# The last of four graph layers rebuilt: its edge keys spread by TensorE and compared on all partitions

## The reference, cut to what matters

```python
h = jnp.maximum(_layernorm(x, axis=-1), 0.0)
x = x + _L3_gnn_ref(h, L3_gnn_rel_embed_weight, L3_gnn_W, src, edge_type_64, dst)

def _L3_gnn_ref(entity_emb, rel_embed_weight, W, heads, rels, tails):
    e_h = entity_emb[heads]
    e_t = entity_emb[tails]
    e_r = rel_embed_weight[rels]                      # 64 relation types
    score = jnp.sum(e_t * jnp.tanh(e_h + e_r), axis=-1)
    score_exp = jnp.exp(score - lax.stop_gradient(jnp.max(score)))
    score_sum = jax.ops.segment_sum(score_exp, heads, num_segments=n_entities)
    attn = score_exp / (score_sum[heads] + 1e-10)
    agg = jax.ops.segment_sum(attn[:, None] * e_t, heads, num_segments=n_entities)
    return jax.nn.leaky_relu((entity_emb + agg) @ W.T, negative_slope=0.2)
```

## Time and profile before

| what | us |
| --- | --- |
| median of 3 runs | 12000.18 |
| lowest and highest of them | 11999.4, 12002.33 |
| the profiled execution | 12014.41 |
| its span in the trace | 12012.6 |
| layer 3's group loop in it, from the last clearing of `a_far` to the last sum | 9146.9 to 11893.4 |

### The profile page before, as it was taken

The page is one execution under the profiler, slowest core; times in us unless marked ns, Lnnn a source line. Parts: engine busy times, 40 slices in busy tenths (PEclk is TensorE's granted clock), DMA queues, the critical chain, the costliest instruction groups (busy, mean ns, idle before and its releaser), DMA issues. The chain is left out here.

```text
span 12012.6 us, 257271 instructions
## 1 busy us (share of the span) xinstructions
PE 8140.2 (68%) x63022; PEld 6349.2 (53%) x63685; DVE 8287.7 (69%) x33874; ACT 4862.3 (40%) x9481; POOL 6896.0 (57%) x7087
## 2 busy tenths in 40 slices
PE   0222222255888888867766777777755999999996
PEld 0222222234566555556545666666653777777775
DVE  7444444426888888878526999999987666666664
ACT  3000000003777777722103555555542444444442
POOL 1777777722777777720004777777753666666662
PEclk9999999998888888889857999999987999999997
DMA  3333333330222222146301222222252333333345
GB/s 116 80 80 80 80 80 80 78 29 24 61 60 59 59 58 58 50 121 175 104 11 34 60 59 60 60 59 60 60 46 64 98 99 98 98 99 98 98 97 59
DMA packets 863125, 886.04 MB, mean 74 GB/s; under 512 B 466669, under 2 KB 636430, under 8 KB 862693
## 3 DMA queue, kind: packets, MB, share of 16 engines
q0 software_dynamic: 254464, 511.95, 18.7%
q1 hardware_dynamic: 608613, 373.57, 12.0%
HBM read 699.65 MB, written 155.84 MB: 71 GB/s over the span
## 5 line engine op out<-in xcount | busy, mean ns | idle before, releaser
L1291 POOL DMA_INDIRECT a_far<-node_table,a_rows x3552 | 3464.3, 975 | 3242.7 <-DMA a_rows<-edge_records 1256.1
L1069 POOL DMA_INDIRECT message_records<-f_msg,f_index x1760 | 1746.3, 992 | 924.2 <-issue 528.1
L897 POOL DMA_INDIRECT sum_far<-split_table,sum_rows x1760 | 1669.2, 948 | 669.4 <-issue 631.9
L982 PE MATMUL banks<-sum_far,sum_hot 128*128 128x128 bf16 x5280 | 635.5, 310 | 1711.8 <-DMA sum_far<-split_table,sum_rows 1604.8
L982 PEld LDWEIGHTS banks<-sum_far,sum_hot 128*128 128x128 bf16 x5280 | 528.2, 143 | 1819.0 <-issue 891.1
L964 ACT ACTIVATE acc<-sum_cur 128x128 f32 x880 | 272.2, 309 | 2752.8 <-DVE sum_cur L926 2415.6
L926 DVE SCALAR_TENSOR_TENSOR sum_cur<-sum_cur,gsame,banks 128x128 f32<-128x128 f32 x880 | 303.0, 344 | 1253.6 <-PE banks L982 1250.5
L1429 PE MATMUL banks<-ident,a_score 128*128 128x128 f32 x7072 | 997.1, 287 | 223.2 <-DVE a_score L1351 197.5
L1449 PE MATMUL banks<-a_far,a_prob 128*128 128x129 f32 x7056 | 1029.6, 291 | 0.0
L1429 PEld LDWEIGHTS banks<-ident,a_score 128*128 128x128 f32 x7072 | 994.5, 202 | 32.3
L1393 ACT ACTIVATE a_hot_t<-banks 128x512 bf16<-128x512 bf16 x888 | 521.4, 587 | 1038.6 <-PE banks L1438 749.9
(11 more groups left out here) (271 smaller groups left out, 19179.5 us busy)
## 6 DMA issues: line engine op xcount, KB each, us to landing
a_rows<-message_records SPq DMA_DIRECT2D x446, 264.0 KB
sum_rows<-message_records SPq DMA_DIRECT2D x441, 264.0 KB
acc<-a_cur SPq DMA_DIRECT2D x880, 65.0 KB
a_far<-node_table,a_rows POOLq DMA_INDIRECT x3552
sum_far<-split_table,sum_rows POOLq DMA_INDIRECT x1760
message_records<-f_msg,f_index POOLq DMA_INDIRECT x1760
f_attr<-edge_attributes SPq DMA_DIRECT2D x447, 40.0 KB
edge_attributes<-in_edge_attr SPq DMA_DIRECT2D x8, 1953.1 KB, 33.7
```

Source lines behind the costliest of these rows:

```text
L897: pool.indirect_dma_start(far[:, u, q, :], None, k.table3[:, :], bass.IndirectOffsetOnAxis(ap=rows[:, u, q, C_SRC:C_SRC + 1].bitcast(I32), ...
L982: last = nc.tensor.matmul(k.psum[a % 2][:, 0:D], hot[:, u, q, :], rhs, start=q == 0 and part == 0, stop=q == KG - 1 and part == (2 if o == ...
L1069: pool.indirect_dma_start(k.mrec[:, :], bass.IndirectOffsetOnAxis(ap=index[:, u, q:q + 1], axis=0), msg[:, u, q, :], None, bounds_check=ED ...
L1291: pool.indirect_dma_start(far[:, u, q, 0:D], None, k.table[:, :], bass.IndirectOffsetOnAxis(ap=rows[:, u, q, other:other + 1].bitcast(I32) ...
```

## The change

`attention(k, 1)` is replaced by a new function, `relation(k)`. All else of the kernel stays, but for the relation table and a few constants made at the start, and `CREDIT`, a constant that all waits and first counts share. In `relation`:

- SP loads only the 4 words behind each message: 512 pieces of 16 bytes a group.
- Heads (`r_rel`) and types (`r_kind`) are made on DVE as before (`columns`, lead 6). PE then writes them along the free axis on all 128 partitions, 8 matmuls with the column, repeated 128 times, as weights and the identity as the moving operand (`spread_keys`, lead 6); ACT copies the 1024 columns as bf16 (`take_keys`, lead 6); DVE compares them with each partition's number, 2 instructions of 512 columns (`one_hots`, lead 5). That gives the turned one-hots at once. Partitions 64 to 127 of the type's one-hot repeat 0 to 63, so that the first two bf16 parts of the relation rows (`rel2`) take one matmul.
- ACT takes the tanh within PSUM, DVE scores from PSUM.
- One running maximum serves all heads of a window: DVE takes the maximum of 4 scores a partition (`r_peak`), PE spreads the 128 of them (1 matmul), DVE takes their maximum.
- ACT takes the exponential of 4 scores a partition. DVE makes weighted one-hots, edges on partitions, 4 instructions with two per-partition operands (`weigh`, lead 1), and PE sums rows by them.
- Slots are 8 deep instead of 4.

The transposes are gone, and `cols_ready`, DVE's last result of the step, releases the matmuls that took their place. ACT does, in this order, the exponentials, the tanh and `take_keys`. The diff, cut to its core:

```diff
--- before.py
+++ after.py
@@ -49,7 +49,7 @@
-CREDIT = 10
+CREDIT = 16
@@ -131,10 +131,12 @@
-        rel_f = sb(top, "rel_f", [NTYPE, D])
-        rel3 = sb(top, "rel3", [NTYPE, 3 * D], BF16)
+        rel_f = sb(top, "rel_f", [P, D])
+        rel2 = sb(top, "rel2", [P, 2 * D], BF16)
+        part_id, part_i = sb(top, "part_id", [P, 2]), sb(top, "part_i", [P, 1], I32)
...
@@ -186,8 +190,13 @@
+                split3(nc, lambda ins: link(dve, ins), rel_hi, rel_mid, rel_lo, rel_f[:, :], relr)
+                nc.vector.tensor_copy(rel2[0:NTYPE, 0:D], rel_hi[0:NTYPE, :])
+                nc.vector.tensor_copy(rel2[NTYPE:P, 0:D], rel_mid[NTYPE:P, :])
+                nc.vector.tensor_copy(rel2[0:NTYPE, D:2 * D], rel_lo[0:NTYPE, :])
...
@@ -258,7 +269,7 @@
-        attention(k, 1)
+        relation(k)
@@ -1482,6 +1493,227 @@
+def relation(k):
+    nc, o = k.nc, 1
+    LOAD, GATHER, COLS, HOT, NEAR, SCORE, MAX, WEIGH, ADD = 7, 6, 6, 5, 4, 3, 2, 1, 0
+    S, H = 2 * U, 4
...
+    with ExitStack() as own:
+        sb = lambda name, shape, dt=F32: k.sb(own, "r_" + name, shape, dt)
+        rows, keys = sb("rows", [P, S, KG, MW - M_SRC], I32), sb("keys", [P, 2, 2, GE], BF16)
+        rel, hide, kind = sb("rel", [P, S, KG]), sb("hide", [P, S, KG]), sb("kind", [P, S, KG])
+        hot_t, kind_t = sb("hot_t", [P, H, GE], BF16), sb("kind_t", [P, H, GE], BF16)
+        far = sb("far", [P, S, KG, XW])
+        work, raw, score, peak = sb("work", [P, KG, D]), sb("raw", [P, KG]), sb("score", [P, S, KG]), sb("peak", [P, S])
+        gmax, before, factor = sb("gmax", [P, 1]), sb("before", [P, S]), sb("factor", [P, S])
+        prob, share = sb("prob", [P, S, KG]), sb("share", [P, 2, KG, P])
+        cur = sb("cur", [P, S, XW])
...
+        near_ps, sum_ps, peak_ps, key_ps = k.psum[0:2], k.psum[2:4], k.psum[4:6], k.banks[:, 6:8, :]
+        top_half = lambda col: col.bitcast(BF16)[:, 1:2].to_broadcast([P, P])
...
+                def load(g, a):
+                    wait(sp, now, prob_ready, g, a, S)
+                    e0 = first_edge(sp, k, o, g + a)
+                    sp.dma_start(rows[:, a % S, :, :], k.mrec[bass.ds(e0, GE), M_SRC:MW].bitcast(I32).rearrange("(p q) c -> p q c", q=KG))\
+                        .then_inc(loads_in[a % S], 16)
+                def keep(g, a):
+                    wait(sp, now, added, g, a)
...
+                skewed(sp, (LOAD, load), (ADD, keep), counts=now, turn=S)
...
+                    pool.wait_ge(loads_in[u], slot_count(now, g, a, 16, S, s_load[u]))
+                    wait(pool, now, summed, g, a, S)
...
+                    for q in range(KG):
+                        pool.indirect_dma_start(
+                            far[:, u, q, 0:D], None, k.table[:, :],
+                            bass.IndirectOffsetOnAxis(ap=rows[:, u, q, M_DST - M_SRC:M_DST - M_SRC + 1], axis=0))\
+                            .then_inc(gathered[u], 16)
+                skewed(pool, (GATHER, gather), counts=now, turn=S)
+            @block.vector
+            def _(dve):
...
+                def columns(g, a):
+                    u = a % S
+                    dve.wait_ge(loads_in[u], slot_count(now, g, a, 16, S, s_load[u]))
+                    nc.vector.tensor_scalar(rel[:, u, :], rows[:, u, :, 0], k.gbase[o][:, bass.ds(g + a, 1)], None, ALU.subtract)
+                    nc.vector.tensor_copy(kind[:, u, :], rows[:, u, :, M_TYPE - M_SRC]).then_inc(cols_ready, 1)
+                    wait(dve, now, cols_ready, g, a)
+                    nc.vector.tensor_scalar(hide[:, u, :], rel[:, u, :], float(P), -BIG, ALU.is_ge, ALU.mult)
+                def one_hots(g, a):
+                    h, b = a % H, a % 2
+                    wait(dve, now, keys_taken, g, a)
+                    wait(dve, now, near_ready, g, a, H)
+                    nc.vector.tensor_scalar(hot_t[:, h, :], keys[:, b, 0, :], k.part_id[:, 0:1], None, ALU.is_equal)
+                    nc.vector.tensor_scalar(kind_t[:, h, :], keys[:, b, 1, :], k.part_id[:, 1:2], None, ALU.is_equal)\
+                        .then_inc(onehotT_ready, 1)
+                def score_edges(g, a):
+                    u, b = a % S, a % 2
+                    dve.wait_ge(gathered[u], slot_count(now, g, a, 16 * KG, S))
+                    wait(dve, now, edge_term, g, a)
+                    wait(dve, now, scores, g, a, 1)
+                    for q in range(KG):
+                        last = nc.vector.scalar_tensor_tensor(
+                            work[:, q, :], near_ps[b][:, q * D:(q + 1) * D], 1.0, far[:, u, q, 0:D], ALU.mult, ALU.mult,
+                            accum_out=raw[:, q:q + 1])
+                    last.then_inc(edge_dot, 1)
+                    wait(dve, now, edge_dot, g, a)
+                    wait(dve, now, weighed, g, a, S)
+                    nc.vector.tensor_tensor(score[:, u, :], raw[:, :], hide[:, u, :], ALU.add).then_inc(masked, 1)
+                    wait(dve, now, masked, g, a)
+                    wait(dve, now, spread, g, a, S)
+                    nc.vector.tensor_reduce(peak[:, u:u + 1], score[:, u, :], AX, ALU.max).then_inc(scores, 1)
+                def running_max(g, a):
+                    u, f = a % S, bass.ds(g + a, 1)
+                    past = cur[:, (u - 1) % S, D + 1:D + 2]
+                    wait(dve, now, exp_in, g, a, 1)
+                    wait(dve, now, shrink, g, a, S)
+                    nc.vector.tensor_scalar(before[:, u:u + 1], past, k.gfresh[o][:, f], None, ALU.add)
+                    wait(dve, now, spread, g, a)
+                    nc.vector.tensor_reduce(gmax[:, :], peak_ps[a % 2][:, 0:P], AX, ALU.max).then_inc(group_max, 1)
+                    dve.wait_ge(kept, now(g, 16 * (a + 1), 16))
+                    wait(dve, now, group_max, g, a)
+                    nc.vector.scalar_tensor_tensor(cur[:, u, D + 1:D + 2], gmax[:, :], -1.0, past, ALU.mult, ALU.min)\
+                        .then_inc(exp_in, 1)
+                def weigh(g, a):
+                    u, b = a % S, a % 2
+                    wait(dve, now, weighed, g, a)
+                    wait(dve, now, summed, g, a, 2)
+                    for q in range(KG):
+                        last = nc.vector.tensor_scalar(share[:, b, q, :], k.iota_b[:, :], rel[:, u, q:q + 1],
+                                                       prob[:, u, q:q + 1], ALU.is_equal, ALU.mult)
+                    last.then_inc(prob_ready, 1)
+                def add(g, a):
+                    u, b = a % S, a % 2
+                    wait(dve, now, summed, g, a)
+                    wait(dve, now, shrink, g, a)
+                    wait(dve, now, added, g, a, 1)
+                    nc.vector.scalar_tensor_tensor(cur[:, u, 0:D + 1], cur[:, (u - 1) % S, 0:D + 1], factor[:, u:u + 1],
+                                                   sum_ps[b][:, 0:D + 1], ALU.mult, ALU.add).then_inc(added, 1)
+                skewed(dve, (HOT, one_hots), (ADD, add), (WEIGH, weigh), (SCORE, score_edges), (MAX, running_max), (COLS, columns),
+                       counts=now, turn=S)
+            @block.scalar
+            def _(act):
...
+                def take_keys(g, a):
+                    wait(act, now, keys_spread, g, a)
+                    wait(act, now, onehotT_ready, g, a, 2)
+                    nc.scalar.activation(keys[:, a % 2, :, :], key_ps, ACT.Copy).then_inc(keys_taken, 1)
+                def terms(g, a):
+                    b = a % 2
+                    wait(act, now, near_ready, g, a)
+                    nc.scalar.activation(near_ps[b], near_ps[b], ACT.Tanh).then_inc(edge_term, 1)
+                def exps(g, a):
+                    u = a % S
+                    wait(act, now, exp_in, g, a)
+                    wait(act, now, prob_ready, g, a, S)
+                    nc.scalar.activation(prob[:, u, :], score[:, u, :], ACT.Exp, bias=cur[:, u, D + 1:D + 2]).then_inc(weighed, 1)
+                    wait(act, now, added, g, a, S)
+                    nc.scalar.activation(factor[:, u:u + 1], before[:, u:u + 1], ACT.Exp, scale=-1.0,
+                                         bias=cur[:, u, D + 1:D + 2]).then_inc(shrink, 1)
+                skewed(act, (MAX, exps), (NEAR, terms), (COLS, take_keys), counts=now, turn=S)
+            @block.tensor
+            def _(pe):
...
+                def spread_keys(g, a):
+                    u = a % S
+                    wait(pe, now, cols_ready, g, a)
+                    wait(pe, now, keys_taken, g, a, 1)
+                    for i, col in enumerate((rel, kind)):
+                        for q in range(KG):
+                            last = nc.tensor.matmul(key_ps[:, i, q * P:(q + 1) * P], top_half(col[:, u, q:q + 1]), k.ident_b[:, :],
+                                                    start=True, stop=True)
+                    last.then_inc(keys_spread, 1)
+                def near(g, a):
+                    h, b = a % H, a % 2
+                    w = window(pe, k, o, g + a)
```

(26 more changed lines are left out.)

64 lines of the change are left out of this document (56 added, 8 removed).

## The result

The changed kernel takes **12,133.3 us** in the median (12,124.4 to 12,138.0, 4 runs), the kernel before in the same comparison 11,999.8 us (11,998.0 to 12,002.3, 4 runs). The ratio is 1.011, 95% interval 1.0093 to 1.0128: slower by 1.1%, 133 us. The prediction had 12,020 us, a range of 11,880 to 12,210 and 0.44 on slower. The profiled execution took 12,124.4 us, span 12,122.7.

What follows compares the result with a forecast made beforehand. DVE's serial path was to replace PE as the bound: 4.07 us own stretch, 1.94 round trip and 0.09 clock make 6.10 us a group against 6.08. With fixed costs, 12,020 us; range 11,880 to 12,210.

Steps and rivals of the forecast that it cites:

- The round trip: Between DVE's columns and one-hots of one group: keys pass through PE and ACT while DVE waits, 1.94 us a group.
- The rival of plain weights: PE's key matmuls load weights at fp32's pace, 0.12 us apart: +0.42, 6.52 us a group, 12,205 us; chance 0.22.
- DVE's stretch: DVE's own work in a step, from one-hots to columns, with waits and register instructions: 4.07 us a group.
- the second operand: DVE's four weighted one-hots: a second per-partition operand costs 0 to 0.24 us a group, taken as 0.12.
- Weighted one-hots 0.26 apart: Sign on DVE that the prediction was wrong; it had counted 0.20 us each, plus 0.12 for all four.
- The clock: TensorE's granted clock in the new loop falls to about 0.91, adding 0.09 us a group.
- The price at half speed: At 1.2 GHz each PE matmul takes 0.05 us more, 0.4 us for the eight key matmuls.
- PE's work: PE's matmuls in the new loop: busy 3.7 us a group, near 65% of the loop.
- Every eighth step has the loop's branch: In DVE's stretch: the branch, a dozen waits and register instructions were together allowed 0.17 us a group.
- The fixed part: Outside the steady groups: one more step of filling, 6 us, and larger slot clearing with setup, 4 us.
- Over two steps of lead: The load of 16-byte pieces was said to have this lead; DVE's columns waiting for it would show the prediction wrong.
- the forecast's own width: 5.98 to 6.22 us a group, 11,967 to 12,073 us, chance 0.47; from the operand, the gaps and the clock.

Runs made afterwards that it cites:

- e8_early_load: Changed kernel with DVE's columns first and one-hots last, five implied waits dropped, loads 8 steps ahead instead of 7: 11,578.7 us, 0.9627 of the kernel before.

## Why the prediction was right, and where it was not

- **The mechanism.** The round trip is there, at the place and with the engines named, and in its step DVE, not PE, is the bound. That it lies on the path is shown by the order alone (5.88 to 4.36 us an undisturbed step, across chips; 6.25 to 4.15 on one chip, with the five waits gone from both), and `e8_early_load`, in which it is off the path, has the group at 5.03 us.
- **The round trip**, 1.94 us, is 1.77. PE's part is 0.62, not 0.74, the hand-over to DVE 0.03, not 0.10; the copy, 1.02, is exact. ACT was to be free 0.2 us before the keys; it is free at the same moment, which costs nothing and leaves nothing. The rival of plain weights fell: 0.057 us between key matmuls.
- **DVE's stretch**, 4.07 us, is 4.12 undisturbed (4.32 from one-hot to the end of `r_hide`, less 0.20 behind the cast). Within it the second operand was mis-sized: 0.06 for each, 0.24 a group, not 0.12. "Weighted one-hots 0.26 apart" was my sign for a wrong step, and they are 0.256 apart. The rest was 0.07 too dear.
- **The clock**, 0.09 us at 0.91, is mis-sized: it is 0.80. In the last four steps of a turn, where the branch is far behind, the round trip takes 1.67 us on the mean against 1.57 at full clock and DVE's stretch 4.39 against 4.32: 0.17 together. The price at half speed, 0.4 for the eight key matmuls, was right: 1.98 against 1.57. What led to 0.91 was PE's work, put at 3.7 us a group and 65% of the loop; it is busy 5.1 us a group (1957 us in 385) and 79%, and still 4.3 in `e8_early_load` at a clock of 0.94.
- **The branch.** "Every eighth step has the loop's branch" was in the sum, under 0.17 for a dozen waits and register instructions. This is the step that failed. A turn's four disturbed steps cost (7.63 + 7.05 + 6.38 + 6.17 - 4 x 6.06) = 2.99 us, 0.37 a group, some 160 us: more than the whole 133 us by which the kernel became slower. About half of it, 1.57, is the stop itself, the rest lies in the steps behind it, mostly with PE at 1.2 GHz. This is worked out from the steps; the changed kernel without the fetch alone was measured only where the kernel before takes 14,460 us or more. Without it the group is at 6.06, against 6.10 predicted. Before the change the same branch took 0.29 us, and no row of the trace of before shows what 22 more instructions do.
- **The sum.** 5.89 + 0.17 + 0.37 = 6.43, measured 6.44; predicted 6.01 + 0.09 = 6.10. The fixed part, +10 us, was some -20: the last 20 groups gave back 13 us, perhaps for want of the large loads, which no run parts from the rest.
- **POOL** was to wait for the sums, about 1 us a group. It waits for the load instead, 458.3 / 280 = 1.64 us. "Over two steps of lead" overlooked that SP issues the load behind the wait for a sum. In the changed kernel that costs nothing: DVE never waits there for a gathered row.
- The time, 12,133, lies outside the forecast's own width (11,967 to 12,073) and inside the range, which the rival of plain weights had stretched to 12,210 for a reason that did not happen. The range held by another's price.

## What to carry to other kernels

Where one engine makes an operand, two others carry it on and the first needs it back, a whole step should lie between, and that is a matter of the order within its step. Count the instructions in an unrolled loop's turn as well: beyond some length the branch fetches code, and dropping waits that others imply can then save more than the waits' own time. An instruction queue that moves packets at every turn, and idle time without a releaser right behind the branch, are the signs. Where a change lifts the bound, look at once at what the next one waits for, above all a small load queued behind a wait for the last result.

## What the hardware showed that I had not expected

- A branch back over 256 instructions of DVE (288 with the reads of the accumulator) took 3.09 us to the next instruction, over 216 or 234 (248 or 266) 0.29. The kernel before, made 32 instructions longer in its turn, lost 1.5% on a chip at 14,500 us.
- In the changed kernel such a stop costs nearly as much again behind it, 1.42 us beside 1.57: the granted clock of TensorE goes from 0.92 at the branch to 0.50 ten us later, and is back after nineteen.
- A second per-partition operand costs a 128-column instruction of DVE 0.06 us (0.256 against 0.196 from start to start).
- Chips differ: with the same kernels and instruction times, three of the chips held loads and engines up for some 5 us of every 15, 14,460 to 14,720 us against 12,000. What does it is not known from these traces.
